# Scan of a spiral recurrence: ScalarE copies the loaded sums into PSUM, TensorE only adds the recurrent rows

## What is computed

```
def step(g, inp):
    ci, ni, nm, nc = inp
    local = g[:, ci, :]
    nb = g[:, ni, :]
    neigh = (nb * nm[None, :, None]).sum(axis=1) / nc
    u = jnp.concatenate([local, neigh], axis=-1)
    y_sc = jnp.tanh(u @ w1 + b1) @ w2 + b2
    g = g.at[:, ci, :].set(local + y_sc[:, None] * w_y[None, :])
    return (g, None)
```

## Time and profile before

| | us |
|---|---|
| median of 3 runs (lowest, highest) | 4998.29 (4994.5, 5005.27) |
| the profiled execution's own time | 5006.68 |
| its span | 5004.8 |

### The profile page before, as it was taken

One profiled execution on the slowest core, in us unless ns is written; L12 is line 12 of the kernel. 1 busy time (PEld: TensorE's weight loads), 2 busy tenths in 40 slices (PEclk: granted clock), 3 DMA queues, 4 the chain that ended last, 5 costly groups with the idle time before them and its releaser, 6 DMA issues.

```text
span 5004.8 us, 62963 instructions
## 1 busy us (share of the span) xinstructions
PE 4586.7 (92%) x20107; PEld 3278.7 (66%) x20107; DVE 4012.3 (80%) x6122; ACT 2289.1 (46%) x3670; POOL 3523.9 (70%) x2480
## 2 busy tenths in 40 slices
PE   3999999999999999999999999988888888887865
PEld 2778888888888888888888887744444444444432
DVE  6888888888887888888888888288888887877753
ACT  2555555555555555555555554343444443333321
POOL 3888888888887888888888888565666655554321
PEclk7999999999999999999999999999999999999985
DMA  3344344434444444343444342499998988876530
GB/s 92 112 131 138 128 138 128 138 128 138 128 138 131 135 128 138 128 138 128 138 128 138 128 138 106 173 315 295 295 313 285 285 271 253 242 222 188 168 108 25
DMA packets 395138, 835.35 MB, mean 167 GB/s; under 512 B 76864, under 2 KB 178496, under 8 KB 394688
## 3 DMA queue, kind: packets, MB, share of 16 engines
q1 hardware_dynamic: 251408, 420.08, 30.5%
q0 software_dynamic: 143408, 411.26, 22.0%
HBM read 419.95 MB, written 425.85 MB: 169 GB/s over the span
## 4 chain that ended last, share of the span: by engine, by line
PE 69%; DVE 11%; issue 11%; POOL 4%; ACT 3%; DMA 2%; SPq 0%; another core or an unknown queue 0%; POOLq 0%; DVEq 0%; ACTq 0%
PE psum L849 14%; PE psum L851 14%; PE psum L850 14%; PE psum L833 13%; PE psum L862 5%; DVE psum L706 4%; PE psum L820 3%; DVE dw_rows L714 3%; POOL out L463 2%; ACT psum L539 2%; PE psum L871 2%; PE psum L831 2%; PE psum L881 1%; DMA out<-dw_rows 1%; DVE near L706 1%
## 5 line engine op out<-in xcount | busy, mean ns | idle before, releaser
L631 DVE SCALAR_TENSOR_TENSOR dw_rows<-relu_rows,taps,dw_rows 128x1792 f32<-128x1792 f32 x872 | 1803.1, 2079 | 25.0 <-ACT dw_rows L516 19.7
L444 POOL DMA_INDIRECT s_x<-xo,wave_idx x784 | 1440.3, 1837 | 315.0 <-issue 213.1
L463 POOL DMA_INDIRECT out<-dw_rows x897 | 891.2, 993 | 870.7 <-DVE dw_rows L714 497.7
L849 PE MATMUL psum<-w_hi,u_hi 128*128 128x512 f32 x3136 | 1384.7, 442 | 0.0
L450 POOL DMA_INDIRECT s_pre<-eo,wave_idx x784 | 1170.3, 1493 | 246.7 <-issue 207.3
L851 PE MATMUL psum<-w_hi,u_lo 128*128 128x512 f32 x3136 | 1234.6, 394 | 0.0
L850 PE MATMUL psum<-w_lo,u_hi 128*128 128x512 f32 x3136 | 1221.1, 389 | 0.0
L481 ACT ACTIVATE eo<-psum 128x512 f32<-128x512 f32 x784 | 468.6, 598 | 1495.6 <-PE psum L851 1417.2
L862 PE MATMUL psum<-dw_rows,ident 128*128 128x512 f32 x1794 | 979.9, 629 | 165.3 <-DVE near L706 104.3
L539 ACT ACTIVATE psum<-psum 128x512 f32<-128x512 f32 x897 | 522.1, 582 | 916.7 <-PE psum L871 468.1
L706 DVE CUSTOM_DVE_ANT_0 psum<-psum,dw_rows,b_col 128x512 f32<-128x512 f32 x897 | 678.2, 756 | 204.6 <-ACT psum L539 145.8
(11 more groups left out here) (95 smaller groups left out, 3886.0 us busy)
## 6 DMA issues: line engine op xcount, KB each, us to landing
dw_rows<-s_pre SPq DMA_DIRECT2D x615, 256.0 KB
x_tok<-x SPq DMA_DIRECT2D x112, 896.0 KB
dw_rows<-s_x SPq DMA_DIRECT2D x615, 128.0 KB
dw_rows<-s_pre SPq DMA_DIRECT2D x169, 192.0 KB
dw_rows<-s_x SPq DMA_DIRECT2D x169, 96.0 KB
out<-dw_rows POOLq DMA_INDIRECT x897
s_x<-xo,wave_idx POOLq DMA_INDIRECT x784
s_pre<-eo,wave_idx POOLq DMA_INDIRECT x784
```

Source lines behind the costliest of these rows:

```text
L444: pool.indirect_dma_start(s_x, bass.IndirectOffsetOnAxis(wave_idx[:, n:n + 1], 0), xo[:, n % XO_SLOTS, :], None, bounds_check=TILES * P - ...
L463: pool.indirect_dma_start(out_rows, bass.IndirectOffsetOnAxis(store_idx[:, c:c + 1], 0), o_t[:, c % OUT_SLOTS, :], None, bounds_check=OUT_ ...
L631: dve.scalar_tensor_tensor(out=dst, in0=pair_rows(relu_rows, k + ky - 1, c, 2 * kx * NB), scalar=taps[:, c, 3 * ky + kx:3 * ky + kx + 1], ...
L849: pe.matmul(bank, hi, w_hi[:, k, :], start=k == 0, stop=False)
```

## The change

The hand-over moves from TensorE to ScalarE: a Copy activation from `pre_t` into the PSUM bank, with the same two waits, again 4 tiles ahead and in front of the tanh of tile c. TensorE keeps `add_sums` and the turns. `add_sums(c)` adds onto data that ScalarE has written, and waits for `passed` of its tile. A matmul that adds (start=False) needs the bank marked as written by TensorE; for that TensorE writes each of the six banks once at the start (`primed`), and ScalarE's first copy waits for it.

```diff
@@ scalar engine
             last.then_inc(v_ready, 1)
+            act.wait_ge(primed, 1)
+
+            def hand_over(c):
+                act.wait_ge(pre_in[c % PRE_SLOTS], 16 * (c // PRE_SLOTS + 1))
+                if c >= BANKS:
+                    act.wait_ge(y_ready, c - BANKS + 1)
+                act.activation(psum[:, c % BANKS, :], pre_t[:, c % PRE_SLOTS, :], ACT.Copy).then_inc(passed, 1)
+
+            for c in range(AHEAD):
+                hand_over(c)
             for c in range(TILES):
+                if c + AHEAD < TILES:
+                    hand_over(c + AHEAD)
                 act.wait_ge(pre_ready, c + 1)
@@ tensor engine
             pe.wait_ge(hid_copied, TILES1)
             pe.wait_ge(xp_copied, TILES1)
-
-            def hand_over(c):
-                pe.wait_ge(pre_in[c % PRE_SLOTS], 16 * (c // PRE_SLOTS + 1))
-                if c >= BANKS:
-                    pe.wait_ge(y_ready, c - BANKS + 1)
-                pe.matmul(psum[:, c % BANKS, :], ident[:, :], pre_t[:, c % PRE_SLOTS, :], start=True,
-                          stop=False).then_inc(passed, 1)
+            for b in range(BANKS):
+                last = pe.matmul(psum[:, b, :], ident[:, :], v_rows[:, :], start=True, stop=True)
+            last.then_inc(primed, 1)
...
+                pe.wait_ge(passed, c + 1)
+
                 pe.matmul(psum[:, c % BANKS, :], s_rows[:, part, :], v_sel[:, row, :], start=False,
-                          stop=True).then_inc(pre_ready, 1)
+                          stop=True, skip_group_check=True).then_inc(pre_ready, 1)
...
-            for c in range(AHEAD):
-                hand_over(c)
             for c in range(TILES):
-                if c + AHEAD < TILES:
-                    hand_over(c + AHEAD)
                 add_sums(c)
```

More of the change, by code:

```diff
@@ L338, in build @@
         xt_in = [sem(f"xt_in{i}") for i in range(XT_SLOTS)]
+        primed = sem("primed")
         passed = sem("passed")
```

## The result

The change makes the kernel slower: 5117.05 us median against 5001.78 of the kernel before, run beside it, a ratio of 1.0232 (95% interval 1.0213 to 1.0251), some 115 us. The forecast was 5075 in a range of 4990 to 5120. The profiled execution has a span of 5115.5 us.

The account below looks back on a forecast made before the run. It took the loop of dot product, hand-over, matmuls and turn as the bound, and expected TensorE at half clock: scan 1834 against 1756.1 us, +78, less 1, gives 5084 profiled, median 5075; range 4990 to 5120, own range 5040 to 5110.

Parts of the forecast that it names:

- The sum: Scan's seven stages added up at half clock: 1834 against 1756.1 us, +78, then -1 for the start.
- shares of 35 to 41%: TensorE's expected busy share without hand-overs in full-clock stages (52% with two tiles), compared with a 40% stretch before half clock.
- rival 1: Whole scan: the clock stays at 2.4 GHz, gaining 138 us, to 4860; chance 0.08.
- Rivals 1 and 2: Scan's clock: stays at 2.4 GHz, 4860, chance 0.08; or goes back and forth, 4970 or 5032, chance 0.13.
- rival 4: DMA alone rules: first two stages stand still, the rest as in the sum, 5060; counted in the forecast's 0.70.
- four-step chain through the turn: Last dot product of a part to the dot product two tiles on: 3.90 us at half clock, or 3.98.
- Stalls for DMA about 5: Stages of 7 and 6 tiles: about 5 us of stalls added to each stage's chain.
- -7 for the clock: Stage of 7 tiles: matmuls piling up behind a turn may lift the clock now and then, -7 us.
- L871 alone at half clock: Adding matmul's start to tanh: 0.75 instead of 0.53 us at half clock, ends 0.53 and 1.26.
- Rival 3: ScalarE is the next bound, by copies at 0.71 or waiting ahead of tanh and L544: 5125; chance 0.09.
- Here the copy itself is in the chain: Stage of 3 tiles: the copy on ScalarE lengthens the chain by about 0.1 to 0.6 us.
- bound of 10.6 us a level by DMA: Stage of 7 tiles at full clock: DMA's share of 0.93 of 11.4 us asks for 10.6 a level.

Follow-up runs that it names:

- e2_slots: The changed kernel with 8 instead of 4 output slots; 5076.56 us, ratio 1.0159 to the kernel before.
- e4_fill_slots: The changed kernel with one float32 matmul of zeros per tile on TensorE and 8 output slots; 4868.93 us, ratio 0.9742 to the kernel before.
- e7_light_fill: e4_fill_slots with each matmul of zeros as a single float32r one, 0.21 instead of 0.85 us at full clock; 4933.56 us, ratio 0.9873 to the kernel before.
- e1_fill: The changed kernel with one float32 matmul of zeros per tile put back on TensorE, still 4 output slots; 4955.65 us, ratio 0.9918 to the kernel before.
- e6_more_fill: e4_fill_slots with a second matmul of zeros per tile in the stage of one tile a level; 4828.97 us, ratio 0.9665 to the kernel before.
- e3_tiny: The changed kernel with ScalarE's copy cut to one element, loaded sums left out of the result; 5113.94 us, ratio 1.0237 to the kernel before.

## Why the prediction was right, and what it missed

**The number.** The direction and the mechanism came out, the size less well. The sum had 77 us for the whole program and 115 were measured. 5117 lies 7 us above the forecast's own range (5040 to 5110) and 3 us inside the stated one.

**The clock.** Expected near 0.5 in the scan, measured 0.54 to 0.50. By the pair e2_slots and e4_fill_slots, which differ in matmuls of zeros alone, the clock costs 5076.56 - 4868.93 = 208 us, what the matmuls of zeros themselves take already subtracted. The outcome is the one that the earlier trace rows pointed to, in each stage. The working behind it was thinner than it looks: its shares of 35 to 41% are over the lengths before the change. Over rival 1's lengths at a full clock they are about 40 to 45% (96 of 211 us with 4 tiles), at or above the one stretch of 40% that fell, and e7_light_fill shows that the share alone does not decide. The Trainium skill (TensorE: Matmul & The Clock Gate, "Part 1: The HAM clock gate") has the throttled state as the default that activity lifts; e1_fill and e7_light_fill agree, the first with 0.98 and up in six stages, the second with 0.68 to 0.99 in the same six.

**The rivals.** Rivals 1 and 2 are out by the clock, rival 4 by the first two stages, which did not stand still but are 11 and 23 us longer. Rival 1's number, 4860, is near e4_fill_slots (4869), but by luck. That kernel has 8 slots; with the 4 of the change and the clock up (e1_fill) it is 4956. And stage by stage two errors cancel: rival 1 had some 345 us in the first stage, by the wrong bound for DMA, where 316.8 were measured, and some 143 in the last, where the clock did not hold and 185.2 were measured. With the clock up there too (e6_more_fill) it is 4829.

**The chains at half clock.** Per stage, forecast and measured us: 7 tiles 361 and 381.7; 6 tiles 330 and 338.0; 5 tiles 293 and 291.1; 4 tiles 258 and 257.3; 3 tiles 229 and 230.3; 2 tiles 188 and 193.3; 1 tile 175 and 176.6. The four-step chain through the turn (3.90 and 3.98 us) is right within 1% in the stages of 5 and 4 tiles.

**What was mis-sized.** The sum said +78 and the profiles differ by 5115.5 - 5004.8 = 111. The term that failed is "Stalls for DMA about 5" with 7 and 6 tiles (with the -7 for the clock): 29 of the 34 us between the sum's 1834 and the 1868.3 of the windows are there. Beyond 32 times the chain it put -2 and 5 us, and 19 and 13 were measured (381.7 - 363, 338.0 - 325). I took the stalls of the kernel before and did not ask what the new rhythm does to the slots. With the adding matmuls free of `y_ready`, three or four tiles follow a turn 1.1 us apart (3455.05, 3456.11 in the trace), while GpSimd starts a store every 1.3 us (3458.63, 3459.91); four slots run out, and VectorE waits in front of the very operations that feed the next turn. e2_slots took 42 us off these two stages; that is more than the 29 missing there, since with the slots the first stage runs 11 us under its chain at half clock and the second needs no stalls at all. The -7 for the clock had the right sign. The second term is L871 alone at half clock: 0.75 was put, 0.83 measured, 5 us in the stage of 2 tiles and 1 to 2 in those of 3 tiles and of 1. It lay well inside its ends of 0.53 and 1.26.

**Rival 3 and the 3-tile chain.** "Here the copy itself is in the chain" was wrong (e3_tiny); the length of 7.12 us came out right within 1% because the turn's end lies at the same place; that is luck. Rival 3's total of 5125 is nearer to the measured 5117 than the forecast is, and its cause, the copies, is out by e3_tiny: luck too. The copy was put at 0.60 and measures 0.596.

**DMA.** The bound of 10.6 us a level by DMA was wrong, by e4_fill_slots (9.90); the forecast's sum did not use it.

## What to carry to other kernels

Work that leaves TensorE can take its clock with it: before moving matmuls off the engine, work out its busy share stage by stage and compare it with stretches of the trace at either clock. That is a warning and no sure forecast (e7_light_fill). One matmul of zeros per tile brought the clock back here in six stages of seven; in the last it took two per tile. When a wait goes away and tiles start to come in bursts, count the buffers behind the burst anew. And judge such a change at equal clock: here it is 2.3% slower as it stands and 2.3% faster (4868.93 to 4986.05) with the clock and the slots equal, in a kernel that has kept as many large matmuls on TensorE.

## What the runs showed of the hardware

- ScalarE started a tanh 0.52 us behind a copy whose record lasts 0.60 us (4579.91 and 4580.43 in the changed kernel), so copy and tanh together took 1.07 us a tile (3455.95 to 3457.02) and not 0.60 + 0.55.
- Where a single adding matmul of 128x512 was alone, it took from its start to the tanh behind it 0.53 us at 2.4 GHz and 0.83 us at 1.2 GHz; a turn 0.90 and 1.52 to 1.60.
- DMA's share of 0.93 was no sign of a limit: 302 GB/s stood beside it before, and the same transfers reached 352 GB/s at 1.01 in e4_fill_slots.
- Matmuls whose stationary operand is all zeros hold the clock up: 0.54 to 0.50 without them, 0.98 to 1.00 with them in the first six stages (after, e1_fill).
